# Remaining features in quarters of the array, and the normalised x made from x by features and a norm row that goes through DRAM

## What is computed

```python
normed = gamma * x / norm(x) * 128 ** 0.5
q, k, v = heads of normed @ w_q, normed @ w_kv       # 8 heads of 16; q scaled by 1/4
q, k = [1, q, q (x) q / 2 ** 0.5], the same of k      # second Taylor expansion
kv_state = einsum('bhnd,bhne->bhde', k, v)            # sums over the tokens
den = einsum('bhnd,bhd->bhn', q, sum of k over n)
out = einsum('bhnd,bhde->bhne', q, kv_state) / max(den, 1e-5)
x = layernorm(x + out @ w_out)
h = silu((x @ w1.T) * s1) * ((x @ w2.T) * s2)
h = gelu((h @ h1.T) * t1);  h = gelu((h @ h2.T) * t2)
x = layernorm(x + (h @ w3.T) * s3)
```

## Time and profile before

| | us |
|---|---|
| median of 3 runs (582.96 to 585.39) | 583.84 |
| the profiled run, its time | 585.66 |
| the profiled run, its span in the profile | 583.9 |
| one steady step (from 288.27 to 321.97) | 33.70 |

### The profile page before, as it was taken

One profiled execution on the slowest core, in us unless ns is written; L12 is line 12 of the kernel. 1 busy time (PEld: TensorE's weight loads), 2 busy tenths in 40 slices (PEclk: granted clock), 3 DMA queues, 4 the chain that ended last, 5 costly groups with the idle time before them and its releaser, 6 DMA issues.

```text
span 583.9 us, 11628 instructions
## 1 busy us (share of the span) xinstructions
PE 554.3 (95%) x3730; PEld 414.3 (71%) x3730; DVE 479.5 (82%) x1008; ACT 465.2 (80%) x954; POOL 145.9 (25%) x215
## 2 busy tenths in 40 slices
PE   3869999999999999999999999999999999999994
PEld 2436786768778686868868686877868687786772
DVE  3675878989798898979799897979989897978664
ACT  4837797887969798896979888797988879797773
POOL 3431232123133213213222221412322141210000
PEclk9987999999999999999999999999999999999997
DMA  8000000000000000000000000000000000000000
GB/s 285 4 21 1 18 1 2 19 20 18 20 18 18 0 18 18 18 18 18 18 0 18 18 18 18 18 18 5 13 18 18 18 18 18 1 19 1 19 2 36
DMA packets 7366, 12.34 MB, mean 21 GB/s; under 512 B 816, under 2 KB 1840, under 8 KB 7344
## 3 DMA queue, kind: packets, MB, share of 16 engines
q1 hardware_dynamic: 7056, 11.93, 6.2%
q10 hardware_dynamic: 288, 0.13, 0.1%
HBM read 7.86 MB, written 4.19 MB: 21 GB/s over the span
## 4 chain that ended last, share of the span: by engine, by line
PE 83%; issue 3%; DVE 2%; ACT 1%; POOL 0%; POOLq 0%; DVEq 0%
PE fps L408 25%; PE fps L409 25%; PE ring L348 5%; PE ring L331 5%; PE ring L376 5%; PE ring L384 4%; PE ring L308 4%; PE ring L392 2%; PE ring L315 2%; PE fps L448 1%; PE ring L298 1%; PE fps L400 1%; DVE h L878 1%; PE ring L334 1%; PE ring L366 1%
## 5 line engine op out<-in xcount | busy, mean ns | idle before, releaser
L408 PE MATMUL fps<-hid_hi,w_hi 128*128 128x512 f32 x576 | 226.6, 393 | 2.1 <-DVE hid_lo L892 1.4
L409 PE MATMUL fps<-hid_lo,w_hi 128*128 128x512 f32 x576 | 226.4, 393 | 0.0
L408 PEld LDWEIGHTS fps<-hid_hi,w_hi 128*128 128x128 f32 x576 | 108.2, 188 | 26.3 <-DVE hid_lo L892 3.7
L665 ACT ACTIVATE hid_hi<-fps,col 128x512 fp32r<-128x512 f32 x128 | 88.2, 689 | 45.4 <-PE fps L409 45.0
L409 PEld LDWEIGHTS fps<-hid_lo,w_hi 128*128 128x128 f32 x576 | 108.3, 188 | 22.5
L892 DVE TENSOR_TENSOR hid_lo<-fps,hid_hi 128x512 fp32r<-128x512 f32 x128 | 88.2, 689 | 26.3 <-ACT fps L666 23.4
L617 ACT ACTIVATE phiT<-ring 128x512 f32<-128x512 f32 x128 | 73.7, 598 | 15.9 <-PE ring L331 15.9
L666 ACT ACTIVATE fps<-fps,col 128x512 f32<-128x512 f32 x128 | 84.5, 660 | 0.0
L878 DVE SCALAR_TENSOR_TENSOR h<-fps,col,gate_zo 128x512 f32<-128x512 f32 x64 | 47.9, 748 | 35.9 <-ACT gate_zo L652 32.5
L247 DVE TENSOR_TENSOR phi_k<-phi_k 128x896 f32<-128x896 f32 x64 | 69.6, 1092 | 2.2 <-ACT v_one L589 1.7
L1032 POOL TENSOR_TENSOR k_mid<-phi_k,v_one 128x256 f32<-128x256 f32 x32 | 21.5, 673 | 160.4 <-ACT v_one L589 157.4
(11 more groups left out here) (102 smaller groups left out, 911.0 us busy)
## 6 DMA issues: line engine op xcount, KB each, us to landing
x_b<-in_x SPq DMA_DIRECT2D x16, 256.0 KB, 2.6
out<-gate_zo SPq DMA_DIRECT2D x16, 256.0 KB, 2.0
w_raw<-in_h SPq DMA_DIRECT2D x2, 1024.0 KB, 9.1
w_raw<-in_w SPq DMA_DIRECT2D x3, 256.0 KB, 4.1
sel_raw<-in_sel SPq DMA_DIRECT2D x1, 384.0 KB, 5.8
w_qkv_raw<-in_w_kv SPq DMA_DIRECT2D x1, 128.0 KB, 2.8
const<-in_consts ACTq DMA_DIRECT2D x1, 115.0 KB, 3.0
w_qkv_raw<-in_w_q SPq DMA_DIRECT2D x1, 64.0 KB, 3.5
```

Of the source, the lines that this page charges most:

```text
L408: nc.tensor.matmul(fps[:, bank, :], w_hi[:, o:o + P], hi, start=start, stop=False)
L409: return nc.tensor.matmul(fps[:, bank, :], w_hi[:, o:o + P], lo, start=False, stop=stop)
L665: nc.scalar.activation(hid[1 - layer][0][:, m, :], fps[:, bank, :], ACT.Gelu, scale=scale)
```

## The change

x is given to the kernel a second time by features (`xT`, made on the host as an input layout). SP loads it into `x_cols`. The norms `rn` of item t+1 are stored to a small DRAM tensor `rn_rows` and read back as one row of 512 numbers into all 128 partitions (`rn_row`); POOL multiplies both into `xn`, which now has features on the partitions, so `transpose_x` goes (it stays for item 0). ACT and DVE read `xn` from SBUF.

The heads of q are ordered otherwise, so that the rest sums of two heads of each group fill one tile of 128 rows: rest0 and rest1, one matmul and one square each, with the linear features in it as (q + 1) squared; the state's rest is changed to match (`k_small` subtracts 1/2 and a half sum). `q_linear` goes. `apply_rest` has four matmuls of 64 rows and 64 columns. The rest of the state is one transpose.

```diff
 RING = (
-    ("stateT", MIDDLE, 0), ("restT", MIDDLE, 1), ("xT", FRONT, 2), ("acc0", MIDDLE, 0), ("acc1", MIDDLE, 1),
+    ("stateT", MIDDLE, 0), ("restT", MIDDLE, 1), ("acc0", MIDDLE, 0), ("acc1", MIDDLE, 1),
     ("kv0", FRONT, 3), ("kv1", FRONT, 2), ("kv2", FRONT, 3), ("out", MIDDLE, 0), ("qT", FRONT, 1), ("kv3", FRONT, 2),
-    ("sq0", FRONT, 3), ("sq1", FRONT, 0), ("sq8", FRONT, 2), ("sq2", FRONT, 1), ("sq3", FRONT, 3), ("sq4", FRONT, 0),
-    ("sq5", FRONT, 2), ("state", FRONT, 1), ("sq6", FRONT, 3), ("sq7", FRONT, 2))
+    ("sq0", FRONT, 3), ("sq1", FRONT, 0), ("rest0", FRONT, 2), ("sq2", FRONT, 1), ("sq3", FRONT, 3), ("sq4", FRONT, 0),
+    ("rest1", FRONT, 2), ("sq5", FRONT, 0), ("state", FRONT, 1), ("sq6", FRONT, 3), ("sq7", FRONT, 2))
...
+                    if is_positive(t):
+                        sp.wait_ge(xn_ready, t + 1)
+                    sp.dma_start(x_cols[:, :], xT[bass.ds(t + 1, 1)].rearrange("b d n -> (b d) n"))\
+                        .then_inc(cols_loaded, 16)
+                    sp.wait_ge(rn_ready, t + 2)
+                    sp.dma_start(rn_d, rn[:, :]).then_inc(rn_stored, 16)
+                    sp.wait_ge(rn_stored, 16 * (t + 1))
+                    sp.dma_start(rn_row[:, :], rn_all).then_inc(rn_row_loaded, 16)
...
+            def rest_of_q(t, g):
+
+                wait_q_lo(t, g)
+                bank_wait(RING, ring_free, t, f"rest{g}")
+                nc.tensor.matmul(ring[:, bank_of(RING, f"rest{g}"), :], sel[:, 4 * P:5 * P], qT[g][:, :],
+                                 start=True, stop=True).then_inc(ring_full, 1)
...
+            def apply_rest(t):
+                for g in range(2):
+                    rows = slice(64 * g, 64 * g + 64)
+                    for q in range(2):
+                        heads = slice(64 * q, 64 * q + 64)
+                        mm = nc.tensor.matmul(ring[heads, bank_of(RING, f"acc{g}"), :], w_rest[rows, heads],
+                                              restq[q][rows, :], start=False, stop=True)
                     mm.then_inc(ring_full, 1)
...
             def x_hi(t):
-                act.wait_ge(ring_full, written(RING, t, "xT"))
-                nc.scalar.activation(xnT_hi[:, :], ring[:, bank_of(RING, "xT"), :], ACT.Copy).then_inc(x_hi_ready, 1)
+                if is_step(t, 0):
+                    act.wait_ge(x0T_full, 1)
+                else:
+                    act.wait_ge(xn_ready, t + 1)
+                nc.scalar.activation(xnT_hi[:, :], ring[:, X0T, :] if is_step(t, 0) else xnT, ACT.Copy)\
+                    .then_inc(x_hi_ready, 1)
...
+            def square_rest(t, g):
+                bank = bank_of(RING, f"rest{g}")
+                act.wait_ge(ring_full, written(RING, t, f"rest{g}"))
+                nc.scalar.activation(restq[g][:, :], ring[:, bank, :], ACT.Square, bias=shift_c)\
+                    .then_inc(ring_free[bank], 1)
...
-            def q_linear(t):
-
-                bank = bank_of(RING, "qT")
-                nc.vector.tensor_copy(restq[0][0:64, :], ring[0:64, bank, :])
-                nc.vector.tensor_copy(restq[1][64:P, :], ring[64:P, bank, :]).then_inc(ring_free[bank], 1)
...
+            def normed_cols(t):
+
+                pool.wait_ge(cols_loaded, 16 * t)
+                pool.wait_ge(rn_row_loaded, 16 * t)
+                pool.wait_ge(x_lo_ready, t)
+                by_token = [part.rearrange("d (p j) -> d j p", j=NT) for part in (x_cols[:, :], rn_row[:, :])]
+                nc.gpsimd.tensor_tensor(xn[:, :, :], *by_token, ALU.mult).then_inc(xn_ready, 1)
...
-                nc.gpsimd.tensor_tensor(k_mid[:, :, :, :], k, half_sum, ALU.subtract).then_inc(k_mid_ready, 1)
+                half_sum, ones = (v_one[:, j0:j0 + 2, :, n] for n in (SIG, DEN))
+                nc.gpsimd.tensor_tensor(k_half[:, :, :], half_sum, neg_half[:, 0:2].unsqueeze(2).to_broadcast([P, 2, H]),
+                                        ALU.subtract).then_inc(k_half_ready, 1)
+                nc.gpsimd.tensor_tensor(phi_k[:, j0:j0 + 2, :, ONE], ones, half_sum, ALU.subtract)
+                pool.wait_ge(k_half_ready, 2 * t + pair + 1)
+                nc.gpsimd.tensor_tensor(k_mid[:, :, :, :], k, k_half[:, :, :].unsqueeze(3).to_broadcast([P, 2, H, DH]),
+                                        ALU.subtract).then_inc(k_mid_ready, 1)
```

More of the change, by code:

```diff
@@ L276, in _ @@
             sp.dma_start(sel_raw[:, :], sel_d).then_inc(sel_loaded, 16)
-            peeled(step, 0)
+            sp.dma_start(x_b[1][:, :, :], x_d[1]).then_inc(x_loaded[1], 16)
             load_ffn_weights(1, (oh1, h1t))
@@ L466, in step @@
                         transpose_rest(t)
[L467 to L468 removed]
+                    if is_step(t, 0):
+                        transpose_x0()
                     if ffn:
@@ L785, in x_lo @@
             def x_lo(t):
-                bank = bank_of(RING, "xT")
                 dve.wait_ge(x_hi_ready, t + 1)
-                nc.vector.tensor_tensor(xnT_lo[:, :], ring[:, bank, :], xnT_hi[:, :].bitcast(F32), ALU.subtract)\
-                    .then_inc(ring_free[bank], 1)
+                nc.vector.tensor_tensor(xnT_lo[:, :], ring[:, X0T, :] if is_step(t, 0) else xnT,
+                                        xnT_hi[:, :].bitcast(F32), ALU.subtract).then_inc(x_lo_ready, 1)
             def q_lo(t):
@@ L1059, in step @@
                     spread_rest(t)
+                if front and not is_step(t, 0):
+                    normed_cols(t)
                 if front:
@@ L1100 @@
     data["scales"] = _np.concatenate([c.reshape(-1, 128).T for c in columns], axis=1)
-    row = _np.arange(128)
-    head = row[:, None] // 32 == _np.arange(4)[None, :]
+    row, f = _np.arange(128)[:, None], _np.arange(128)[None, :]
+    rest = _np.arange(REST)[None, :]
+    scale = _np.where(rest == ONE - MAIN, 1.0, 0.5)
+    part = f % 32
+    is_one, is_lin = part == ONE - MAIN, (part >= LIN - MAIN) & (part < REST)
     data["consts"] = _np.concatenate([
-        _np.eye(128), _np.repeat(head, DH, axis=1), _np.repeat(head, 8, axis=1) * 0.5, _np.full((128, 4), -0.5),
-        _np.where(row < DH, 1.0, 0.5)[:, None], _np.isin(row, (32, 96))[:, None],
+        _np.eye(128), *((row // 32 % 2 == j) * scale for j in range(2)), _np.full((128, 4), -0.5),
+        _np.where(row < DH, 1.0, 0.5), (is_one | is_lin).T,
     ], axis=1).astype(_np.float32)
-    of_head, e = (row % 64 // DH)[:, None], (row % DH)[:, None]
-    f = _np.arange(128)[None, :]
+    of_head, e = row % 64 // DH, row % DH
     pairs = (e == f % DH) | (e == (f + f // DH) % DH)
     sums = [(of_head == hh) & pairs for hh in range(4)]
-    for at in (64, 0):
-        g = f - at
-        sums.append((g >= 0) & (g < 32) & (of_head == g // 8) & (e % 8 == g % 8))
+    eighth = (part < 8) & (e % 8 == part)
+    sums.append((of_head == f // 32) & (eighth | is_lin & (e == part - (LIN - MAIN))))
     data["sel"] = _np.concatenate(sums, axis=1).astype(_np.float32)
```

175 lines of the change are left out of this document (89 added, 86 removed).

## The result

| | before | after |
|---|---|---|
| median of the runs, us | 583.63 (582.96 to 585.39, 4 runs) | 620.71 (619.52 to 622.49, 4 runs) |
| profiled execution, us | 585.66, span 583.9 | 619.97, span 618.2 |
| steady step, us | 33.71 | 36.26 |

The ratio is 1.064 (95% interval 1.061 to 1.067). The forecast was 587.7 with a range up to 602, so the sign was right and the size far off. In the experiments the kernel before ran beside each variant, at 583.8 to 585.0 us; ratios are always against those runs.

The account below looks back on a forecast made before the run. Two equally long loops bound the kernel: TensorE's, and one through gelu, xnT_hi and hid_lo. 13 steps x 0.31 = 4.0 us, start +0.6, step 2 -0.2, step 16 -0.5: +3.9 on 583.84 gives 587.7 us, range 578 to 602.

Parts of the forecast that it names:

- What bounds the kernel: Steady step: TensorE's loop and a gelu, xnT_hi, hid_lo loop are equally long; what moves xnT_hi moves the step.
- The quarters run side by side: In apply_rest: four matmuls on four quarters take two rounds, 0.86 us less, with about 0.1 us for the switch.
- sq5 in bank 0: TensorE waits 0.48 us for ScalarE's read of sq4; by this alone the loop is 0.1 us longer.
- ScalarE's part: ScalarE's stretch up to xnT_hi: 0.35 us shorter by fewer squares and a narrower copy, if no stall counts.
- The start of the trip: End of the sum of squares on VectorE: 0.88 us earlier, at 319.27 in place of 320.15.
- A: Stretch of a steady step from the start of xnT_hi to the end of the sum of squares: 27.2 us.
- The norm row's trip: From sum of squares through rn, store, row load and multiply to xnT_hi: ends at 326.07, loop 0.3 us longer.
- How often and the start: The longer loop is paid 13 times, 4.0 us; the start adds 0.6 us of a 2.8 us delay.
- The trip is hidden, bank 0 sets the step: Rival: short store and load hide the trip, the sq5 stall adds 0.1 us a step: 585 us, chance 0.2.
- ScalarE's shorter stretch counts: Rival: trip hidden and no stall at sq5, 0.4 us less in each of 13 steps: 578.5 us, chance 0.12.
- rival A of e1: Experiment's rival: with no norm row to wait for, ScalarE's shorter stretch shows, about 578 us; no chance given.
- The slow row load: Rival: 16 DMA engines read the same 2 KB; each us beyond 2.6 costs 13 us, 614 at 4.6; chance 0.13.

Follow-up runs that it names:

- e2: Kernel before with the x half alone (x by features, norm row through DRAM); squares and rest features as before: 632.9 us.
- e6: Changed kernel, but the row load reads one row of x by features 128 times, a row the kernel never writes: 620.8 us.
- e11: Changed kernel with sq5 in PSUM bank 3 in place of bank 0, nothing else: 622.4 us.
- e8: Changed kernel with the norm row loaded once, the multiply without steps of four, and sq5 in bank 3: 577.5 us.
- e9: Changed kernel without its x half (x transposed as before), quarters kept, sq5 in bank 3: 571.9 us.
- e7: Changed kernel with the norm row loaded once (no store or row load in a step), multiply without steps of four, sq5 in bank 0: 584.1 us.
- e1: Changed kernel without its x half (x transposed as before), quarters kept, sq5 in bank 0: 579.3 us.
- e3: Changed kernel, but the load behind the store takes 128 different rows of x by features: 612.8 us.
- e4: Changed kernel, but GpSimd's multiply reads both operands in memory order, not in steps of four elements: 611.3 us.

## Why the prediction was wrong, step by step

**What bounds the kernel** held. What moves `xnT_hi` moves the step: it does so in the changed kernel, e2 to e6 and e11, and TensorE's work alone brings nothing (e8 against e9).

**TensorE.** The quarters run side by side: the new `apply_rest` starts at 311.97 and the next matmuls at 312.99, so 1.02 us in place of 1.72, where I had 0.86 plus 0.1 for the switch. The four independent tiles that the forecast took from the Trainium skill, "TensorEngine Tiling (Array Packing)", agree with this; the price of the switch can't be read off by itself.

**sq5 in bank 0.** The stall is there, put down to ScalarE's read of sq4 (0.30 us at 301.43, 0.33 to 0.36 us of idle time before `copy_y`), and has its size: 0.4 us a step between e7 and e8. What failed is the next sentence, that the loop would be 0.1 longer than before. With no trip it is 0.3 us **shorter** (33.71 to 33.41 in e1), and in bank 3 0.7 shorter. ScalarE's part was nearly right. From the square of sq0, in front of which it waits for TensorE, to the next `xnT_hi` it takes 15.03 us before (310.72 to 325.75), 15.17 in e1 and 14.78 in e9: 0.14 longer with the stall, as forecast, and 0.25 shorter without it, where I had 0.35. What I took as unchanged is VectorE's stretch from `xnT_lo` to the fourth `hid_lo`, since its work is. It is 0.35 shorter: 309.61 - 292.73 = 16.88 before, 299.82 - 283.29 = 16.53 in e9 and the same in e1. The other 0.1 is between that `hid_lo` and the square. ScalarE in e1, then ScalarE and VectorE in e9:

```profile
304.99 0.60 ACT L643 ACTIVATE phiT<-ring 128x512 f32<-128x512 f32 x1 [1.11 <-PE ring L346]
...
320.16 0.65 ACT L622 ACTIVATE xnT_hi<-ring 128x512 fp32r<-128x512 f32 x1
```

```profile
300.83 0.60 ACT L643 ACTIVATE phiT<-ring 128x512 f32<-128x512 f32 x1 [1.09 <-PE ring L346]
...
315.61 0.65 ACT L622 ACTIVATE xnT_hi<-ring 128x512 fp32r<-128x512 f32 x1
```

```profile
283.29 0.69 DVE L817 TENSOR_TENSOR xnT_lo<-ring,xnT_hi 128x512 fp32r<-128x512 f32 x1 [0.27 <-ACT xnT_hi L622]
...
299.82 0.69 DVE L915 TENSOR_TENSOR hid_lo<-fps,hid_hi 128x512 fp32r<-128x512 f32 x1
```

The multiply by `rden` in VectorE's stretch lasts 0.92 us before and 0.69 in e1 and e9 (below), which is 0.23 of the 0.35; the other 0.12 is a gap before the third `hid_lo` that I can't explain.

**The start of the trip** held: A, taken from the forecast as 27.2, is 27.37.

**The norm row's trip** is the step that failed: the mechanism is the forecast's, and two terms of its sum were too small, the row load and the multiply. From the sum of squares to `xnT_hi` I had 6.80 us and it is 8.81:

| term | forecast us | measured us | difference |
|---|---|---|---|
| to GpSimd, `rn` | 1.09 | 1.12 | +0.03 |
| SyncE, store of 2 KB, SyncE | 1.94 | 1.43 | -0.51 |
| row load, to GpSimd | 2.68 | 4.11 | +1.43 |
| multiply, to ScalarE | 1.09 | 2.15 | +1.06 |

Store and load together take 5.5 us; I had said that over 5 would prove me wrong. (SyncE's two waits, 0.17 each in the sum, hardly show: the store goes out 0.02 us after `rn`.) The load was taken by its shape on the SBUF side; what it reads counts as well, by e3 and e6 for 0.6 to 0.7 of the 1.4 us, and the other half, which 128 different rows have too, stays without a cause. I had named this rival with 13% and no row above 2.6, and a bound of 2.6 plus "may be slower" is no bound. The multiply was the plain error: "its inputs now have steps of four; no reason for a gain" looked for a gain alone. No row of before showed GpSimd with steps, so both signs were open, and the range should have been widened on the long side; e4 puts 0.84 of the difference on the steps. The rule on steps over 8 bytes (the Trainium skill, "GPSIMD Engine Reference", section 7, above) would have put half of the 1.04 of the earlier trace rows on the multiply, an estimate of 0.5 us a step and 7 us in all. The 2.0 us of fixed cost that I had set beside the store (the Trainium skill, "DMA: Bandwidth & Descriptors"; the section is on DMAs that GpSimd issues, and these are SyncE's) is above the 1.4 that the trace shows for most of the stores.

**How often and the start.** I multiplied by 13; there are twelve full steps and a start. For the start I put 0.6 us of the 2.8 by which the second item's `xnT_hi` would be late. It was 3.33 late (30.26 against 26.93), and none of it was covered: the third is 3.37 late (59.55 against 56.18). The 2.8 has a slip in it: the terms of the trip behind `rn` add up to 5.7, not 6.0, and the 29.7 that follows is right by 5.7 alone. Behind the last `xnT_hi` the kernel is 0.5 us shorter, as much as I had given step 16.

So of the 30.4 us between 3.9 forecast and 34.3 measured, 12 x (2.55 - 0.31) = 27 are the trip with its two mis-sized terms, and 3.5 the start (3.8 more than forecast, less the 0.3 of the one step that I had counted too many).

**The rivals.** "The trip is hidden, bank 0 sets the step", 585 us: e7 has 584.1. "ScalarE's shorter stretch counts", 578.5: e8 has 577.5. Both numbers are luck in part: the first had the step 0.1 us longer than before, and it is 0.3 shorter; the second had it 0.4 shorter and it is 0.7. The same goes for rival A of e1, 578 us by ScalarE's shorter stretch: e1 has 579.3 with a stretch of ScalarE that is 0.14 longer. The slow row load, each us beyond 2.6 for 13: it was 1.3 beyond, about as much as the multiply was. Together with the multiply this reaches beyond the 602 of the range. The range failed because the two unbounded prices were not added at their long ends.

**The signs.** ScalarE's idle time before `xnT_hi`, put down to GpSimd's `xn`, is there, with 2.1 us, not 0.2 to 1; so are `xn` waiting for the row, the short `apply_rest`, the stall at sq5 and a TensorE that is no longer busy all the step.

## What to carry to other kernels

A step that leaves the chip and comes back is a chain of several fixed prices, and in a loop without slack every one of them is paid each time; first ask whether its input exists earlier. Here the same trip costs 37 us at the end of the step and, with the sum of squares 4.8 us earlier in it, nothing in a steady step, since x had been loaded long before. When one engine's operation is replaced by one on data laid out otherwise, price the new layout on that engine, with a long end as well as a short one. And a change of two halves should be timed by halves: one of them was a gain of 1% (2% with a better bank) that the other hid.
